# Attention scores: three PSUM banks for the row maxima, and the subtraction of the maxima in 32-row products at the ends of each burst

## The chip, the cores and the metric

One Trainium2 chip (trn2), one core of it. The metric is the device time of one execution in microseconds (us); the kernel before is given by the median of three runs.

## The reference, cut to what matters

x has 8 batches of 1024 rows of 256; there are 16 heads of 64 (DHEAD).

```python
def _L0_attn_ref(x, gamma, Wq, Wkv, W_bilinear, Wo):
    ...
    q = apply_rotary(q, cos, sin) * DHEAD ** (-0.5)
    k = apply_rotary(k, cos, sin)
    kt = jnp.einsum('bhnd,hde->bhne', k, W_bilinear)
    sim = jnp.einsum('bhid,bhjd->bhij', q, kt)
    attn = jax.nn.softmax(sim, axis=-1)
    out = jnp.einsum('bhij,bhjd->bhid', attn, v)
    ...
x = x + _L0_attn_ref(_layernorm(x, axis=-1), ...)
x = x + _L0_ffn_ref(_layernorm(x, axis=-1), ...)
```

## The kernel before, in words

The program has four parts: the weights are prepared, the input is normalised and turned, the attention runs (most of the time), and a feed-forward part ends it. The change lies in the attention, in `attention()`.

Attention works on pairs of heads, T = 64 pairs (8 batches of 8 pairs). The two heads of a pair lie in partitions 0-63 and 64-127 (`rows(e)`), so that two products of 64 rows, one for each head, can run side by side. The order of work is written out by hand: each engine has its own list, `span(k, t, b)`, and engines meet only in semaphores. A span does three things at once for three different pairs: the attention of pair t (`attn`), the row maxima of pair t+1 (`prep`), and the projections of pair t+2 (`proj`). `pairs` puts spans 1 to 56 in a loop of eight spans per turn.

A span has four quarters q. On TensorE a quarter is:

- a burst over four key tiles n = 4q to 4q+3. For each tile and each head e there are four products into a scores bank S[e][n % 2] (`score`, parts 0 to 3): q_hi with k_hi, q_hi with k_lo, q_lo with k_hi, and `neg_max` with `ones_rows`, which subtracts the maxima (L624). For the next pair there is one product each into X[0] or X[1] (`max_score`, L641), whose row maximum VectorE takes from the bank (L562). A bank X[e] is free again when VectorE has reduced it.
- projections (q = 0 keys, 1 queries, 2 values, L692 and L707) or, at q = 3, the bilinear product of the keys (L721), the first half into bank M ("shared" in the rows), the second into X[0], and at q = 3 also the turning of the maxima (L725) into X[1];
- at q = 0 and 2 the sums of the probabilities over partitions (`sums`, L647, bank M), and always the four tiles' products with the values (L753), called PV below.

ScalarE (ACT) makes the probabilities (`exp`, L491) as soon as a scores bank is complete. At q = 3 it makes, behind the last `exp`, in this order: q_hi (L506), the first half of k_hi (L511), the high part of the maxima (L517), the second half of k_hi. GpSimd (POOL) adds the probabilities over tiles (L435), adds the swapped halves for the rotary embedding (L441) and scales the output (L447).

The maxima of a pair lie in a column layout. Their high and low parts (`nmt`, "neg_max_parts") are made at the end of span t-1, and SyncE (SP) copies them by DMA into rows of `NM` ("neg_max"): row 64e + part. The product of L624 waits for these DMAs at n = 0 (`nm_in`):

```python
for part, made in enumerate((nm_hi, nm_lo)):
    wait(sp, made, t + 2)
    at_rest()
    for e in two:
        row = e * DH + part
        sp.dma_start(NM[(k + 1) % 2][row:row + 1, :].bitcast(F), ...).then_inc(nm_in, 16)
```

Of the kernel before, what the change touches and what calls it, by code (L numbers as in the profile page):

```python
# [12 lines left out]
P = 128  # L13
# [256 lines left out]
def attention(nc, cos_in, sin_in, ident_in, xt_scr, w_scr, wb_scr, z_scr, XT, W, V, cos, next_loads):  # L270
    with ExitStack() as ctx:
# [11 lines left out]
        prob = [sb(f"prob{e}", [P, RING, HALF], F) for e in two]  # L283
        psums = [[sb(f"prob_sum{e}{h}", [P, HALF], F) for h in two] for e in two]
# [21 lines left out]
        exped, x_red, added = per_head("probs_made"), per_head("max_reduced"), per_head("probs_added")  # L306
# [10 lines left out]
        CONSTS = 16 * 4 + 8  # L317
# [24 lines left out]
        def _(sp):  # L342
# [20 lines left out]
            def swap(x, t, c):  # L363
                wait(sp, sin_made[x], 2 * (t + 2) + c + 1)
                at_rest()
                wait(sp, rot_made[x], 2 * (t + 2) + c - 1)
# [50 lines left out]
        def _(pool):  # L417
            for s in added + rot_made + [z_made]:
                pool.sem_inc(s, CREDIT)
# [3 lines left out]
            def add(t, n):  # L423
# [3 lines left out]
                for e in (1, 0):  # L427
                    wait(pool, exped[e], 16 * t + n + 1)
                    if j == 1:
                        wait(pool, l_made, 4 * (t - 1) + 2 * half + 2)  # L430
                        a = prob[e][:, (n - 1) % RING, :]
                    else:
                        wait(pool, added[e], 14 * t + adds_by(n - 1))
                        a = psums[e][half][:, :]
                    nc.gpsimd.tensor_tensor(psums[e][half][:, :], a, prob[e][:, n % RING, :], ALU.add).then_inc(added[e], 1)  # L435

            def rope(t, x, c):
                done = 2 * (t + 2) + c + 1
                wait(pool, swap_in[x][c], 32 * (t + 3))
                wait(pool, cos_made[x], done)  # L440
                nc.gpsimd.tensor_tensor(rot[x][:, cols(c)], rot[x][:, cols(c)], swapped[x][:, cols(c)], ALU.add)\  # L441
                    .then_inc(rot_made[x], 1)
# [6 lines left out]
            def span(k, t, b):  # L449
                attn, prep, proj = has(k)  # L450
                for q in range(QUADS):
                    for jj in range(4):
# [6 lines left out]
                        if proj and q in (1, 2) and jj in (1, 3):  # L459
                            rope(t, q - 1, jj // 2)  # L460
# [4 lines left out]
        def _(act):  # L465
# [10 lines left out]
            def span(k, t, b):  # L476
                attn, prep, proj = has(k)
                u = k % 2
                for q in range(QUADS):
# [4 lines left out]
                    for jj in range(4):  # L484
                        n = 4 * q + jj
                        for e in (1, 0):
                            if attn:
                                wait(act, s_made[e], 16 * t + n + 1)
                                wait(act, pv_made[e], 16 * t + n - RING + 1)
                                wait(act, added[e], 14 * t + adds_by(n) - 7)  # L490
                                nc.scalar.activation(prob[e][:, n % RING, :], S[e][n % 2][:, :], ACT.Exp).then_inc(exped[e], 1)  # L491
# [9 lines left out]
                    if q == 3:  # L501
                        if proj:
                            wait(act, rot_made[Q], 2 * (t + 2) + 2)
# [10 lines left out]
                        if prep:  # L514
                            wait(act, nm_turned, t + 2)
                            wait(act, nm_in, 64 * (t + 1))
# [7 lines left out]
        def _(dve):  # L524
# [4 lines left out]
            for k, p in enumerate(prob):  # L529
                nc.vector.memset(p[:, :, :], 0.0).then_inc(const, 1)  # L530
# [3 lines left out]
            for e in two:  # L534
                nc.vector.memset(onesr[e * DH:e * DH + 2, :].bitcast(F), 1.0).then_inc(const, 1)
# [17 lines left out]
            def span(k, t, b):  # L553
                attn, prep, proj = has(k)
                u = k % 2
                for q in range(QUADS):
                    for jj in range(4):
                        n = 4 * q + jj
                        for e in two:
                            if prep:  # L560
                                wait(dve, x_made[e], 16 * (t + 1) + n + 1)
                                nc.vector.reduce_max(mx[1 - u][:, e, n // 2, n % 2:n % 2 + 1], X[e][:, :], axis=AX.X)\  # L562
# [34 lines left out]
        def _(pe):  # L597
# [3 lines left out]

            def score(t, u, n, e, part):

                half, j = n // 8, n % 8
                out = S[e][n % 2][:, :]
                keys, q = slice(j * P, (j + 1) * P), cols(half)
                if part == 0:
                    wait(pe, exped[e], 16 * t + n - 1)
# [3 lines left out]
                    nc.tensor.matmul(out, KH[u][rows(e), keys], QH[u][rows(e), q], start=True, stop=False)  # L612
# [4 lines left out]
                elif part == 2:  # L617
                    if n == 0:
                        wait(pe, lo_made[Q], t + 1)
                    nc.tensor.matmul(out, KH[u][rows(e), keys], QL[u][rows(e), q], start=False, stop=False)  # L620
                else:
                    if n == 0:
                        wait(pe, nm_in, 64 * (t + 1))
                    nc.tensor.matmul(out, onesr[rows(e), :], NM[u][rows(e), q], start=False, stop=True).then_inc(s_made[e], 1)  # L624

            def max_score(k, t, v, n, e):

                wait(pe, x_red[e], 16 * (t + 1) + n)
                if n == 0:
                    wait(pe, hi_made[K], 2 * (t + 1) + 2)  # L630
                    wait(pe, hi_made[Q], t + 2)
                    wait(pe, lo_made[K], 2 * (t + 1) + 2)
                    wait(pe, nm_lo, t + 1)
                if e == 0 and has(k)[2]:
                    if n == 4 or n == 8:
                        x = n // 4 - 1
                        wait(pe, sin_made[x], 2 * (t + 2) + 2)
                    if n == 12:
                        wait(pe, v_copied, 2 * (t + 2) + 2)
                tile, part = n // 2, n % 2  # L640
                nc.tensor.matmul(X[e][:, :], QH[v][rows(e), tile * P:(tile + 1) * P], KH[v][rows(e), cols(part)],  # L641
                                 start=True, stop=True).then_inc(x_made[e], 1)

            def sums(t, h):
                for e in two:
                    wait(pe, added[e], 14 * t + 7 * h + 7)
                    nc.tensor.matmul(M[rows(e), :], ones[:, :], psums[e][h][:, :], start=True, stop=True).then_inc(l_made, 1)  # L647

            def span(k, t, b):
# [6 lines left out]
                for q in range(QUADS):  # L656
                    for jj in range(4):
                        n = 4 * q + jj
                        if attn:
                            for part in two:  # L660
                                for e in two:
                                    score(t, u, n, e, part)
                        if prep:
                            max_score(k, t, 1 - u, n, 0)
                        if attn:
                            score(t, u, n, 1, 2)
                            score(t, u, n, 0, 2)
                            score(t, u, n, 1, 3)
                            score(t, u, n, 0, 3)
                        if prep:  # L670
                            max_score(k, t, 1 - u, n, 1)

                    if proj and q < 2:
                        for c in two:
                            out = (M if c == 0 else X[0])[:, :]
                            if q == K and c == 0:
# [4 lines left out]
                                wait(pe, hi_made[K], 2 * (t + 1) + 1)  # L681
                                wait(pe, lo_made[K], 2 * (t + 1) + 1)
                            elif q == Q and c == 0:
                                wait(pe, sin_made[K], 2 * pp + 1)
                                wait(pe, inv_made, 2 * (t - 1) + 2)
# [9 lines left out]
                    if proj and q == 2:  # L695
                        for c in two:
                            bank = M if c == 0 else X[0]
                            if c == 0:
                                wait(pe, sin_made[Q], 2 * pp + 1)
# [10 lines left out]
                    if q == 3:  # L710
                        if proj:
                            for c in two:
                                wait(pe, rot_made[K], 2 * pp + c + 1)
                                if c == 0:
                                    wait(pe, v_copied, 2 * pp + 1)
                                    wait(pe, inv_made, 2 * t + 1)
# [10 lines left out]
                    if attn:  # L727
                        if q == 0 and k >= 1:
                            if proj:
                                wait(pe, sin_made[K], 2 * pp + 1)  # L730
                            else:
                                if prep:
                                    wait(pe, lo_made[K], 2 * (t + 1) + 1)
                                wait(pe, inv_made, 2 * (t - 1) + 1)
                            sums(t - 1, 1)
                        if q == 2:
                            if proj:
                                wait(pe, v_copied, 2 * pp + 1)
                            else:
                                wait(pe, inv_made, 2 * (t - 1) + 2)  # L740
                            sums(t, 0)
                        half = q // 2
                        for jj in range(4):
                            n = 4 * q + jj
                            j = n % 8
                            for e in two:
# [6 lines left out]
                                nc.tensor.matmul(O[rows(e), :], V[k // 2 % 2][:, j, col:col + DH], prob[e][:, n % RING, :],  # L753
# [412 lines left out]
```

## Time and profile before

| | |
|---|---|
| median of 3 runs | 4118.36 us (4116.03 to 4121.81) |
| the profiled execution's own time | 4126.92 us |
| its span in the profile | 4124.7 us, mean granted TensorE clock 0.986 |
| TensorE busy | 3712.5 us, 90% of the span |
| VectorE, ScalarE, GpSimd busy | 72%, 42%, 71% |

Attention takes the profile from about 450 to 3520 us, and the pattern of a span repeats in it. TensorE's matmuls are pipelined, so the start of one and the start of the next are the numbers to compare; the duration of one reaches over the start of the next. A granted clock of 1.0 is 2.4 GHz, 0.5 is 1.2 GHz. "issue" is idle time that the profile puts down to no other engine.

### The profile page before, as it was taken

What the parts mean: (1) busy time and instruction counts of PE and PEld (TensorE: products, weight loads), DVE (VectorE), ACT (ScalarE), POOL (GpSimd) and SP (SyncE); (2) the same over time, 40 slices, a digit from 0 to 9 for tenths busy, and PEclk for the clock granted to TensorE, in tenths of its full rate; (3) what the DMA queues carried; (4) which work ended last, traced back from release to release, by engine and by line L of the source; (5) the groups of instructions that cost most, each with busy time, mean ns of one, the idle gap of its engine ahead of it and who ended that gap; (6) DMA issues with size and microseconds to landing.
All of it is one profiled execution on the core that took longest, in us unless ns stands there. A gap on an engine that the chain in (4) does not pass through costs nothing. (4 is left out here: it accounts for less than half of the span.)

```text
span 4124.7 us, 72584 instructions
## 1 busy us (share of the span) xinstructions
PE 3712.5 (90%) x22106; PEld 2378.9 (58%) x22106; DVE 2985.7 (72%) x4457; ACT 1718.4 (42%) x3109; POOL 2915.3 (71%) x2407
## 2 busy tenths in 40 slices
PE   0114999999999999999999999999999999799999
PEld 0002555555655655555555655655656555488888
DVE  4555677777777777677777767776777777399998
ACT  1000344444444444444444444444444444355555
POOL 0111788888888888888888888888888889522221
PEclk9998999999999999999999999999999999899999
DMA  5222111111111111111111111121111101233332
GB/s 203 100 92 111 54 48 70 47 48 52 70 53 48 47 68 47 48 47 70 48 49 51 70 48 52 47 78 48 52 68 50 50 34 46 79 98 93 98 99 72
DMA packets 180740, 273.57 MB, mean 66 GB/s; under 512 B 18720, under 2 KB 113568, under 8 KB 173984
## 3 DMA queue, kind: packets, MB, share of 16 engines
q1 hardware_dynamic: 162720, 244.06, 16.8%
q10 hardware_dynamic: 17664, 25.17, 1.7%
q8 instruction: 174, 2.85, 0.3%
q14 instruction: 182, 1.49, 0.1%
HBM read 131.28 MB, written 69.73 MB: 49 GB/s over the span
## 5 line engine op out<-in xcount | busy, mean ns | idle before, releaser
L435 POOL TENSOR_TENSOR prob_sum<-prob_sum,prob 128x512 f32<-128x512 f32 x1536 | 1983.9, 1324 | 271.5 <-ACT prob L491 269.2
L562 DVE TENSOR_REDUCE row_max<-max_scores 128x1 f32<-128x512 f32 x2048 | 1322.9, 688 | 461.4 <-PE max_scores L641 453.3
L491 ACT ACTIVATE prob<-scores 128x512 f32<-128x512 f32 x2048 | 1111.0, 596 | 1099.2 <-PE scores L624 1083.7
L641 PE MATMUL max_scores<-k_hi,q_hi 64*128 64x512 f32 x2048 | 949.1, 465 | 12.9 <-DVE k_lo L591 4.8
L753 PE MATMUL attn_out<-prob,v 128*64 128x512 f32 x4096 | 929.4, 596 | 0.0
L620 PE MATMUL scores<-q_lo,k_hi 64*128 64x512 f32 x2048 | 641.7, 407 | 0.0
L624 PE MATMUL scores<-neg_max,ones_rows 64*128 64x512 f32 x2048 | 613.9, 400 | 12.5 <-issue 9.3
L541 DVE RECIPROCAL sum_inverted<-shared 128x512 f32<-128x512 f32 x128 | 429.6, 3356 | 256.9 <-PE shared L647 256.7
L753 PEld LDWEIGHTS attn_out<-prob,v 128*64 128x64 f32 x4096 | 285.5, 137 | 561.8 <-issue 560.2
L612 PE MATMUL scores<-q_hi,k_hi 64*128 64x512 f32 x2048 | 514.0, 433 | 8.6 <-issue 7.6
L641 PEld LDWEIGHTS max_scores<-k_hi,q_hi 64*128 64x128 f32 x2048 | 382.5, 187 | 235.5 <-DVE row_max L562 127.6
L616 PE MATMUL scores<-q_hi,k_lo 64*128 64x512 f32 x2048 | 468.4, 396 | 0.0
L435 POOL TENSOR_TENSOR prob_sum<-prob 128x512 f32<-128x512 f32 x256 | 324.4, 1290 | 129.5 <-ACT prob L491 129.5
L624 PEld LDWEIGHTS scores<-neg_max,ones_rows 64*128 64x128 f32 x2048 | 359.8, 187 | 50.8 <-DMA neg_max<-neg_max_parts 15.7
L612 PEld LDWEIGHTS scores<-q_hi,k_hi 64*128 64x128 f32 x2048 | 214.0, 187 | 237.2 <-issue 215.8
L888 POOL TENSOR_TENSOR up_scale<-veps_b,halfpow 128x1 f32<-128x1 f32 x64 | 35.1, 549 | 426.3 <-DVE up_biased L1017 400.9
L620 PEld LDWEIGHTS scores<-q_lo,k_hi 64*128 64x128 f32 x2048 | 321.0, 187 | 12.1
L474 ACT ACTIVATE z_stage<-attn_out 128x512 f32<-128x512 f32 x128 | 76.6, 598 | 545.3 <-PE attn_out L753 541.3
L230 PE MATMUL xt_bank<-ident,x_twice 128*128 128x128 f32 x128 | 31.4, 428 | 278.8 <-DVEq L213 278.8
L616 PEld LDWEIGHTS scores<-q_hi,k_lo 64*128 64x128 f32 x2048 | 253.8, 189 | 10.2
L692 PE MATMUL shared<-xt_batch,w_group 128*128 128x512 f32 x768 | 216.1, 418 | 23.2 <-DMA xt_batch<-x_turned_parts 23.2
L692 PE MATMUL max_scores<-xt_batch,w_group 128*128 128x512 f32 x768 | 198.6, 395 | 0.0
(122 smaller groups left out, 4742.7 us busy)
## 6 DMA issues: line engine op xcount, KB each, us to landing
w_group<-w_parts SPq DMA_DIRECT2D x32, 1536.0 KB, 6.6
k_swapped<-sin_products SPq DMA_DIRECT2D x256, 128.0 KB, 2.1
q_swapped<-sin_products SPq DMA_DIRECT2D x256, 128.0 KB, 2.0
attn_normalised<-z_stage SPq DMA_DIRECT2D x128, 256.0 KB, 2.1
v<-attn_normalised SPq DMA_DIRECT2D x64, 512.0 KB, 4.1
x_turned_parts<-xt_parts ACTq DMA_DIRECT2D x16, 1024.0 KB, 4.5
xt_batch<-x_turned_parts SPq DMA_DIRECT2D x8, 2048.0 KB, 10.7
x_in<-in_x SPq DMA_DIRECT2D x16, 512.0 KB, 3.7
```

Source lines behind the costliest of these rows:

```text
L435: nc.gpsimd.tensor_tensor(psums[e][half][:, :], a, prob[e][:, n % RING, :], ALU.add).then_inc(added[e], 1)
L474: nc.scalar.activation(zst[h][:, :], O[:, :], ACT.Copy).then_inc(z_copied, 1)
L491: nc.scalar.activation(prob[e][:, n % RING, :], S[e][n % 2][:, :], ACT.Exp).then_inc(exped[e], 1)
L541: nc.vector.reciprocal(inv[:, :], M[:, :]).then_inc(inv_made, 1)
L562: nc.vector.reduce_max(mx[1 - u][:, e, n // 2, n % 2:n % 2 + 1], X[e][:, :], axis=AX.X)\
L612: nc.tensor.matmul(out, KH[u][rows(e), keys], QH[u][rows(e), q], start=True, stop=False)
L616: nc.tensor.matmul(out, KL[u][rows(e), keys], QH[u][rows(e), q], start=False, stop=False)
L620: nc.tensor.matmul(out, KH[u][rows(e), keys], QL[u][rows(e), q], start=False, stop=False)
L624: nc.tensor.matmul(out, onesr[rows(e), :], NM[u][rows(e), q], start=False, stop=True).then_inc(s_made[e], 1)
L641: nc.tensor.matmul(X[e][:, :], QH[v][rows(e), tile * P:(tile + 1) * P], KH[v][rows(e), cols(part)], start=True, stop=True).then_inc(x_made ...
L692: last = nc.tensor.matmul(out, w[:, wp, kt, base:base + P], XT[:, xp, kt, cols(c)], start=m == 0, stop=m == len(order) - 1)
L753: nc.tensor.matmul(O[rows(e), :], V[k // 2 % 2][:, j, col:col + DH], prob[e][:, n % RING, :], start=j == 0, stop=j == 7).then_inc(pv_made[ ...
```

## The change

1. `max_score` writes to three banks in turn instead of two: X[0], X[1] and M (`bank_of`). Since M also serves the projections and the sums, TensorE gets new waits on `x_red[1]` before them.
2. Part 3 of `score` goes. In its place `shift` makes the same subtraction with 32 rows for two tiles and both heads, four products in a row on four groups of 32 rows. For the first two tiles of a burst it opens the accumulation (before the scores), for the last two it closes it (behind the last `max_score`). `NM` and `ones_rows` hold the two parts in rows 32g and 32g+1 of all four groups, so there are eight DMAs per pair, not four.
3. The probabilities of both heads lie in one tile; GpSimd adds both heads in one operation of 1024 columns, and the rotary addition takes 1024 columns at once, at jj = 2.

```diff
+        def bank_of(n, e):
+            return (X[0], X[1], M)[(2 * (n % 4) + e) % 3]
...
@@ sync: span
-                        for e in two:
-                            row = e * DH + part
-                            sp.dma_start(NM[(k + 1) % 2][row:row + 1, :].bitcast(F),
-                                         nmt[e * TILES:(e + 1) * TILES, part, :].bitcast(F)).then_inc(nm_in, 16)
+                        for g in two:
+                            row = 32 * g + part
+                            for e in two:
+                                sp.dma_start(NM[(k + 1) % 2][row + e * DH:row + e * DH + 1, :].bitcast(F),
+                                             nmt[e * TILES:(e + 1) * TILES, part, :].bitcast(F)).then_inc(nm_in, 16)
@@ gpsimd: add, rope
-                for e in (1, 0):
+                for e in two:
                     wait(pool, exped[e], 16 * t + n + 1)
...
-                    nc.gpsimd.tensor_tensor(psums[e][half][:, :], a, prob[e][:, n % RING, :], ALU.add).then_inc(added[e], 1)
+                nc.gpsimd.tensor_tensor(psums[half][:, :, :], a, prob[:, n % RING, :, :], ALU.add).then_inc(added, 1)
...
+                nc.gpsimd.tensor_tensor(rot[x][:, :], rot[x][:, :], swapped[x][:, :], ALU.add).then_inc(rot_made[x], 1)
@@ tensor
+            def shift(t, u, n, first):
+                if n == 0:
+                    wait(pe, nm_in, 128 * (t + 1))
+                for m in (n, n + 1):
+                    for e in two:
+                        if first:
+                            wait(pe, exped[e], 16 * t + m - 1)
+                        r = slice(e * DH + 32 * (m % 2), e * DH + 32 * (m % 2) + 32)
+                        last = nc.tensor.matmul(S[e][m % 2][:, :], onesr[r, :], NM[u][r, cols(m // 8)], start=first, stop=not first)
+                        if not first:
+                            last.then_inc(s_made[e], 1)
...
-                    if n == 0:
-                        wait(pe, nm_in, 64 * (t + 1))
-                    nc.tensor.matmul(out, onesr[rows(e), :], NM[u][rows(e), q], start=False, stop=True).then_inc(s_made[e], 1)
+                    last = nc.tensor.matmul(out, KH[u][rows(e), keys], QL[u][rows(e), q], start=False, stop=first)
+                    if first:
+                        last.then_inc(s_made[e], 1)
 
             def max_score(k, t, v, n, e):
-                wait(pe, x_red[e], 16 * (t + 1) + n)
+                i, q, pp = 2 * (n % 4) + e, n // 4, t + 2
+                if i >= 3:
+                    wait(pe, x_red[1 - e], 16 * (t + 1) + 4 * q + (i - 3) // 2 + 1)
...
@@ tensor: span
                         if attn:
-                            for part in two:
+                            if jj == 0:
+                                shift(t, u, n, True)
+                            for part in range(3):
                                 for e in two:
                                     score(t, u, n, e, part)
                         if prep:
-                            max_score(k, t, 1 - u, n, 0)
-                        if attn:
-                            score(t, u, n, 1, 2)
-                            score(t, u, n, 0, 2)
-                            score(t, u, n, 1, 3)
-                            score(t, u, n, 0, 3)
-                        if prep:
-                            max_score(k, t, 1 - u, n, 1)
+                            for e in two:
+                                max_score(k, t, 1 - u, n, e)
+                        if attn and jj == 3:
+                            shift(t, u, n - 1, False)
...
                                 wait(pe, lo_made[K], 2 * (t + 1) + 1)
+                                wait(pe, x_red[1], 16 * (t + 1) + 3)
```

The last added wait stands ahead of the key projection into M; the other projections into M have one like it.

What moves, in the order of the two programs. The subtraction is `scores<-neg_max,ones_rows`, the products for the maxima are `max_scores<-k_hi,q_hi`. TensorE, the last tile of the last burst of a span, before:

```order
L612 MATMUL scores<-q_hi,k_hi 128x512 x2
L616 MATMUL scores<-q_hi,k_lo 128x512 x2
L641 MATMUL max_scores<-k_hi,q_hi 128x512
L620 MATMUL scores<-q_lo,k_hi 128x512 x2
L624 MATMUL scores<-neg_max,ones_rows 128x512 x2
L641 MATMUL max_scores<-k_hi,q_hi 128x512
L721 MATMUL shared<-k_rotated,wb_blocks 128x512
```

TensorE, the same place now:

```order
L629 MATMUL scores<-q_hi,k_hi 128x512 x2
L633 MATMUL scores<-q_hi,k_lo 128x512 x2
L637 MATMUL scores<-q_lo,k_hi 128x512 x2
L675 MATMUL max_scores<-k_hi,q_hi 128x512 x2
L614 MATMUL scores<-neg_max,ones_rows 128x512 x4
L757 MATMUL shared<-k_rotated,wb_blocks 128x512
```

The subtraction for the third and fourth tile (the last x4) now stands behind all eight products of the maxima, directly ahead of the bilinear product. TensorE, the first two tiles of a burst now, behind PV of the burst before:

```order
L791 MATMUL attn_out<-prob,v 64x512 x8
L614 MATMUL scores<-neg_max,ones_rows 128x512 x4
L629 MATMUL scores<-q_hi,k_hi 128x512 x2
L633 MATMUL scores<-q_hi,k_lo 128x512 x2
L637 MATMUL scores<-q_lo,k_hi 128x512 x2
L675 MATMUL max_scores<-k_hi,q_hi 128x512 x2
L629 MATMUL scores<-q_hi,k_hi 128x512 x2
L633 MATMUL scores<-q_hi,k_lo 128x512 x2
L637 MATMUL scores<-q_lo,k_hi 128x512 x2
L675 MATMUL shared<-k_hi,q_hi 128x512
L675 MATMUL max_scores<-k_hi,q_hi 128x512
```

The product that reads `neg_max` has moved from behind three pairs of products to the very front. SP's DMA queue at the end of a span, before:

```order
L406 DMA neg_max<-neg_max_parts 1x8x128 [waits max_hi]
L406 DMA neg_max<-neg_max_parts 1x8x128
L406 DMA neg_max<-neg_max_parts 1x8x128 [waits max_lo]
L406 DMA neg_max<-neg_max_parts 1x8x128
L369 DMA k_swapped<-sin_products 64x512 [waits k_sin_made,k_rot_made]
```

and now:

```order
L411 DMA neg_max<-neg_max_parts 1x8x128 [waits max_hi]
L411 DMA neg_max<-neg_max_parts 1x8x128 x3
L411 DMA neg_max<-neg_max_parts 1x8x128 [waits max_lo]
L411 DMA neg_max<-neg_max_parts 1x8x128 x3
L373 DMA k_swapped<-sin_products 64x512 [waits k_sin_made,k_rot_made]
```

The same queue issues eight DMAs of the same size where it issued four.

## Rows read from the trace of the kernel before

**Rows 1.** Busy time by stretch, steady attention: us, busy us per engine, clock, DMA.

```profile
1000.00:3500.00 2500.00, 2480.18 (x14447) 1479.65 (x14447) 1830.25 (x2381) 1106.48 (x2030) 2195.69 (x1726) 0.99 0.15 53
```

**Rows 2.** Costliest groups, whole profile: line, engine, operation, count, busy, mean ns, idle.

```profile
L435 POOL TENSOR_TENSOR prob_sum<-prob_sum,prob 128x512 f32<-128x512 f32 x1536 | 1983.9, 1324 | 271.5 <-ACT prob L491 269.2
L562 DVE TENSOR_REDUCE row_max<-max_scores 128x1 f32<-128x512 f32 x2048 | 1322.9, 688 | 461.4 <-PE max_scores L641 453.3
```

**Rows 3.** Timeline of TensorE, last burst of a span and the next: start, length.

```profile
1003.62 1.46 PE L753 MATMUL attn_out<-prob,v 128*64 128x512 f32 x6
1005.00 0.50 PE L612 MATMUL scores<-q_hi,k_hi 64*128 64x512 f32 x2
1005.34 0.39 PE L616 MATMUL scores<-q_hi,k_lo 64*128 64x512 f32 x2
1005.57 0.39 PE L641 MATMUL max_scores<-k_hi,q_hi 64*128 64x512 f32 x1
...
1009.90 0.49 PE L641 MATMUL max_scores<-k_hi,q_hi 64*128 64x512 f32 x1
1010.32 1.13 PE L721 MATMUL shared<-k_rotated,wb_blocks 128*128 128x512 f32 x2
...
1012.35 3.65 PE L753 MATMUL attn_out<-prob,v 128*64 128x512 f32 x16
1015.93 0.50 PE L612 MATMUL scores<-q_hi,k_hi 64*128 64x512 f32 x2
...
1016.94 0.50 PE L624 MATMUL scores<-neg_max,ones_rows 64*128 64x512 f32 x2
...
1021.53 0.50 PE L692 MATMUL shared<-xt_batch,w_group 128*128 128x512 f32 x1
```

**Rows 4.** Timeline of TensorE, where the other bursts begin and end.

```profile
1029.09 0.50 PE L612 MATMUL scores<-q_hi,k_hi 64*128 64x512 f32 x2
...
1034.42 1.66 PE L692 MATMUL shared<-xt_batch,w_group 128*128 128x512 f32 x6
...
1040.95 0.50 PE L612 MATMUL scores<-q_hi,k_hi 64*128 64x512 f32 x2
...
1046.29 1.69 PE L707 MATMUL shared<-w_group,xt_batch 128*128 128x256 f32 x12
...
1053.79 0.49 PE L612 MATMUL scores<-q_hi,k_hi 64*128 64x512 f32 x2
```

**Rows 5.** Timeline of VectorE in the last burst of two spans.

```profile
1006.00 5.13 DVE L562 TENSOR_REDUCE row_max<-max_scores 128x1 f32<-128x512 f32 x8 [0.84 <-PE max_scores L641]
...
2046.25 1.29 DVE L562 TENSOR_REDUCE row_max<-max_scores 128x1 f32<-128x512 f32 x2
```

**Rows 6.** Timeline of ScalarE at the end of the span of rows 3.

```profile
1010.16 1.09 ACT L491 ACTIVATE prob<-scores 128x512 f32<-128x512 f32 x2 [0.20 <-PE scores L624]
1011.13 1.06 ACT L506 ACTIVATE q_hi<-q_rotated 128x1024 fp32r<-128x1024 f32 x1
1012.08 0.60 ACT L511 ACTIVATE k_hi<-shared 128x512 fp32r<-128x512 f32 x1
1012.55 0.25 ACT L517 ACTIVATE neg_max_parts<-max_scores 16x128 fp32r<-16x128 f32 x1
```

**Rows 7.** The DMAs of the maxima: SP's issues, all issues (ns min/median/max), who waits.

```profile
1012.90 2.88 SPq L406 DMA_DIRECT2D neg_max<-neg_max_parts  x4
...
L406 SPq DMA_DIRECT2D neg_max<-neg_max_parts x256: 623/655/2701, 420.5 to 3520.8; - x128
...
1016.93 0.19 PEld L624 LDWEIGHTS scores<-neg_max,ones_rows 64*128 64x128 f32 x2 [0.25 <-DMA neg_max<-neg_max_parts]
```

**Rows 8.** Timeline of TensorE at a turn of the loop.

```profile
2052.93 0.60 PE L612 MATMUL scores<-q_hi,k_hi 64*128 64x512 f32 x2 [0.50 <-issue]
...
2056.18 0.58 PE L624 MATMUL scores<-neg_max,ones_rows 64*128 64x512 f32 x1 [1.89 <-issue]
...
2062.95 0.51 PE L692 MATMUL shared<-xt_batch,w_group 128*128 128x512 f32 x1
```

**Rows 9.** Busy time by stretch at the same place, columns as in rows 1.

```profile
2055.00:2062.00 7.00, 5.82 (x27) 5.62 (x28) 3.28 (x5) 2.55 (x6) 2.19 (x2) 0.53 0.02 6
```

More of the change, by code:

```diff
@@ L282, in attention @@
         WB = sb("wb_blocks", [P, PAIRS, P], F)
-        prob = [sb(f"prob{e}", [P, RING, HALF], F) for e in two]
-        psums = [[sb(f"prob_sum{e}{h}", [P, HALF], F) for h in two] for e in two]
+        prob = sb("prob", [P, RING, 2, HALF], F)
+        psums = [sb(f"prob_sum{h}", [P, 2, HALF], F) for h in two]
         prod = sb("sin_products", [P, N], F)
@@ L365, in swap @@
                 at_rest()
-                wait(sp, rot_made[x], 2 * (t + 2) + c - 1)
+                wait(sp, rot_made[x], t + 2)
                 at_rest()
@@ L426, in add, with rope @@
                     return
-                for e in (1, 0):
+                for e in two:
                     wait(pool, exped[e], 16 * t + n + 1)
[L429 to L434, printed above, removed]
-                    nc.gpsimd.tensor_tensor(psums[e][half][:, :], a, prob[e][:, n % RING, :], ALU.add).then_inc(added[e], 1)
[L437 to L442, printed above, removed]
+                if j == 1:
+                    wait(pool, l_made, 4 * (t - 1) + 2 * half + 2)
+                    a = prob[:, (n - 1) % RING, :, :]
+                else:
+                    wait(pool, added, 14 * t + adds_by(n - 1))
+                    a = psums[half][:, :, :]
+                nc.gpsimd.tensor_tensor(psums[half][:, :, :], a, prob[:, n % RING, :, :], ALU.add).then_inc(added, 1)
+            def rope(t, x):
+                for c in two:
+                    wait(pool, swap_in[x][c], 32 * (t + 3))
+                wait(pool, cos_made[x], 2 * (t + 2) + 2)
+                nc.gpsimd.tensor_tensor(rot[x][:, :], rot[x][:, :], swapped[x][:, :], ALU.add).then_inc(rot_made[x], 1)
             def norm_z(t, h):
@@ L533, in _ @@
             dve.wait_ge(zeroed, 1)
-            for e in two:
-                nc.vector.memset(onesr[e * DH:e * DH + 2, :].bitcast(F), 1.0).then_inc(const, 1)
+            for g in range(4):
+                nc.vector.memset(onesr[32 * g:32 * g + 2, :].bitcast(F), 1.0).then_inc(const, 1)
             dve.wait_ge(const, CONSTS)
@@ L607, in score @@
                 if part == 0:
-                    wait(pe, exped[e], 16 * t + n - 1)
+                    if not first:
+                        wait(pe, exped[e], 16 * t + n - 1)
                     if n == 0:
@@ L611, in score @@
                         wait(pe, hi_made[K], 2 * t + 2)
-                    nc.tensor.matmul(out, KH[u][rows(e), keys], QH[u][rows(e), q], start=True, stop=False)
+                    nc.tensor.matmul(out, KH[u][rows(e), keys], QH[u][rows(e), q], start=not first, stop=False)
                 elif part == 1:
@@ L630, in max_score @@
                     wait(pe, hi_made[K], 2 * (t + 1) + 2)
-                    wait(pe, hi_made[Q], t + 2)
                     wait(pe, lo_made[K], 2 * (t + 1) + 2)
+                elif q == 0 and i == 1:
                     wait(pe, nm_lo, t + 1)
[L634 to L639, printed above, removed]
+                elif q and i == 1:
+                    wait(pe, x_red[1], 16 * (t + 1) + 4 * q)
+                elif q and not proj:
+                    wait(pe, x_red[i // 2], 16 * (t + 1) + 4 * q - i // 2)
+                    if q == 1 and i == 2:
+                        wait(pe, inv_made, 2 * (t - 1) + 2)
+                    if q == 3 and i == 2:
+                        wait(pe, inv_made, 2 * t + 1)
+                elif q and i == 0:
+                    if q < 3:
+                        wait(pe, sin_made[q - 1], 2 * pp + 2)
+                    else:
+                        wait(pe, v_copied, 2 * pp + 2)
+                elif q == 1:
+                    wait(pe, sin_made[K], 2 * pp + 1)
+                    wait(pe, inv_made, 2 * (t - 1) + 2)
+                elif q == 2:
+                    wait(pe, sin_made[Q], 2 * pp + 1)
+                elif q == 3:
+                    wait(pe, v_copied, 2 * pp + 1)
+                    wait(pe, inv_made, 2 * t + 1)
@@ L640, in max_score @@
                 tile, part = n // 2, n % 2
-                nc.tensor.matmul(X[e][:, :], QH[v][rows(e), tile * P:(tile + 1) * P], KH[v][rows(e), cols(part)],
+                nc.tensor.matmul(bank_of(n, e)[:, :], QH[v][rows(e), tile * P:(tile + 1) * P], KH[v][rows(e), cols(part)],
                                  start=True, stop=True).then_inc(x_made[e], 1)
@@ L645, in sums @@
                 for e in two:
-                    wait(pe, added[e], 14 * t + 7 * h + 7)
-                    nc.tensor.matmul(M[rows(e), :], ones[:, :], psums[e][h][:, :], start=True, stop=True).then_inc(l_made, 1)
+                    wait(pe, added, 14 * t + 7 * h + 7)
+                    nc.tensor.matmul(M[rows(e), :], ones[:, :], psums[h][:, e, :], start=True, stop=True).then_inc(l_made, 1)
             def span(k, t, b):
@@ L698, in span @@
                             if c == 0:
-                                wait(pe, sin_made[Q], 2 * pp + 1)
+                                if not prep:
+                                    wait(pe, sin_made[Q], 2 * pp + 1)
+                                wait(pe, x_red[1], 16 * (t + 1) + 11)
                             else:
```

52 lines of the change are left out of this document (27 added, 25 removed).

## The prediction

> **What bounds the kernel now.** I read the busy time by stretch first. In steady attention TensorE is busy for 2480.18 of 2500 us, POOL for 2195.69 and VectorE for 1830.25 [rows 1]: whatever makes TensorE stand still is paid in full, and what POOL and VectorE save is worth nothing by itself. Then TensorE's timeline shows where its time goes. A span is 48.79 us, from the last burst of one (1005.00) to that of the next (1053.79) [rows 3, 4]. The bursts take 5.32 (q = 3), 5.60 (q = 0), 5.33 and 5.34 us, each from its first product to the first projection [rows 3, 4]; projections, sums and PV between them take 7.56, 6.53 and 7.50 us. A burst isn't a stream of products alone: VectorE reduces its eight maxima in 5.13 us almost without a pause [rows 5]. So inside a burst VectorE and TensorE are about level.
>
> The chain at the end of a span comes third. The last `exp` pair starts 5.16 us into the last burst, then q_hi, k_hi, the maxima's high part at 12.55 [rows 6], and SP's four DMAs from 12.90 on [rows 7]. The weight load of the subtraction in the next burst starts at 1016.93, after 0.25 us of idle time that the DMA ended [rows 7]. That is 1.00 us after the burst's first product [rows 3]: the maxima already come just in time, and only because three pairs of products stand ahead of the one that reads them.
>
> **The change, part by part.** *Slots removed.* Pairs of products start 0.23 us apart (1005.34 to 1005.57) [rows 3]. A burst has 20 such slots; now it has 16, and two for the subtractions if four products of 32 rows run as two of 64 rows do. 2 x 0.23 x 4 bursts would be 1.8 us a span, if slots bound the burst.
>
> *What bounds the new burst.* The first product of a burst starts 0.52 us after the last pair of PV (PV pairs are 0.43 apart, so the third of the row of six is at 1004.48), and the next slot comes 0.34 behind it. The first projection comes 0.42 us behind the last product for the maxima (1009.90, 1010.32) [rows 3]. Where the array changes from one shape to another, a slot of 0.23 becomes about 0.42 and the one behind it 0.34. The new burst has two more such places, 32 to 64 rows at its start and 64 to 32 at its end. No row shows 32 rows; between 0 and 0.30 us a place, I take what these rows show. The Trainium skill says the same of this change (TensorEngine Tiling (Array Packing), "Key Properties": switching the tiling mode drains the array, switching the tile doesn't). By that rule the burst below is 5.63 us; if a switch between 32 and 64 rows cost nothing, 5.20.
>
> From the burst's start: scores at 0.42, 0.76 and 0.99, the first maxima at 1.22. VectorE starts 0.43 after its product (1005.57 to 1006.00) [rows 3, 5], so at 1.65, and back to back one reduction follows another in 0.60 (1.29 less 0.69) [rows 2, 5]. With three banks the eighth product needs the fifth reduction: 1.65 + 4 x 0.60 + 0.69 = 4.74, so it starts at 4.79. The closing subtraction starts at 5.21, the projection at 5.63. Its bank M is free at 1.65 + 5 x 0.60 + 0.69 = 5.34, so the new wait on M is covered, but only by 0.3 us. So the burst does not get shorter, it grows: the first maxima stand one slot and one change of shape later than before (1.22 against 0.57). Three bursts, 16.89 us, replace 16.27: **+0.6 us** up to the last burst.
>
> *The closing subtraction on ScalarE.* Third and fourth tile are complete only at the burst's end: 5.21 + 0.50 + 0.11 gives 5.82 for the first of four `exp`, 0.49 apart, so the last pair starts at 6.80 and not at 5.16. Everything behind it on ScalarE, k_hi and the high part of the maxima, is late by **1.64 us**. PV needs these tiles only after two pairs of it; that is covered.
>
> *Four more DMAs.* The four take 2.88 us with a last one of 0.66, so 0.74 each [rows 7]. They are issued one after another on SP: four more are **+2.96 us**. Bounds: 0.62 (the shortest issue) to 0.80 each. From the last issue (1012.90 + 2.88 - 0.66 = 1015.12) to the weight load there are 1.81 us, unchanged. What stands behind them on SP, a store of z and the next swap (needed some 9 us into the next span), is covered by its own distance.
>
> *The subtraction in front.* Before, the load came 11.93 us after the start of the last burst, and the next burst began at 10.93. Now it comes at 11.93 + 1.64 + 2.96 = 16.53, and the burst begins with it. That step is +5.60 us, and with +0.62 the span is 55.0 us: **+6.2 us**. TensorE stands still for about 5.3 us in each, since PV ends 3.6 us after 7.7. 63 such steps are 391 us.
>
> *The clock.* At a turn of the loop TensorE idles for 1.89 us and more, and then the granted clock is 0.53 of full for 7 us, its lower level [rows 8, 9]; that burst took 10.02 us, of which 2.3 between two products of one pair, so 7.7 against 5.60 [rows 3, 8]. An idle time of 5.3 us should do so in every span. If the low level reaches 3 us into the burst, the first maxima come 1 us later and VectorE passes that on; if over the whole burst, it costs 2.5. I take **1.5 us**, 95 us in all. The turns of the loop lie inside the new wait now, and their low clock is already counted: 7 x 4.4 = 31 us back.
>
> *POOL.* One operation of 1024 columns for two of 512: between 2 x 1.32 [rows 2] and about half. POOL has idle time and gets more of it, since the span grows; I take nothing. Without that cover it would be the sums at q = 0 and 2 that wait. Rotary additions in one piece, at jj = 2: needed at q = 3, nothing. The larger constants at the start: under 2 us, nothing.
>
> Sum: 391 + 95 - 31 = 455 us on the profiled execution's 4126.92, 4582; the median lies 8.6 below that execution. **4575 us**, 11% slower.
>
> **Rivals.** *A: no cost of shape.* The Tiling page would be wrong for 64 to 32 rows. Bursts 5.20, closing subtraction at 4.83: 3 x 0.43 + 0.38 = 1.67 us less a span, 4470 us. For it: both shapes keep all 128 columns. Against it: every change the rows show has its gap.
>
> *B: the clock holds.* Then 95 us go: 4480. Against it stand rows 8 and 9, with less than half the idle time.
>
> *C: the clock is low over the whole next burst.* 2.5 us a span and not 1.5: 4640.
>
> *D: four products of 32 rows don't run together,* but in two pairs. Then each burst has two more slots of 0.23: about 1.6 us a span over three and a half bursts, 4675.
>
> *E: the maxima arrive in time after all,* if the eight DMAs are issued beside each other or PV hides them. Then bursts decide, and by A's 5.20 they are 0.2 us shorter than before: 4 x 0.2 x 63 = 50 us, **4068 us, faster**. It decides where the last DMA lands within 11.2 us of the last burst's start; the sum has it at 16.5, and the four of today land at 11.9. All that speaks for it is the count of slots.
>
> *F: gain and loss cancel,* within 0.2%, which is about what a measurement of this kernel can tell from no change. No row leads there.
>
> **How the numbers follow.** Forecast 0.52, A 0.12, B 0.11, C 0.13, D 0.07, E 0.03, F 0.02. The range holds all but E and F and a rest of the tails: from 4440 (A with shorter issues, 0.62 each) to 4690 (D). Faster 0.03, same 0.02, slower 0.95.
>
> **What would show it.** In the profile after: the first waits of a span's first burst are of the subtraction's weight load on the DMA of `neg_max`, some 4 to 6 us in each span, where it was 0.25; SP shows eight issues of 0.7 us; a granted clock that falls once a span; bursts of 5.5 to 5.7 us away from that place, the first reduction 1.6 us after their start; gaps of about 0.42 around the closing four. The forecast is wrong if that load waits less than 2 us, if the span stays below 52 us, or if the bursts fall under 5.2.

## The result, and the profile after

| | before | after |
|---|---|---|
| median | 4117.93 us (4 runs) | 4595.22 us (4594.78 to 4597.28, 4 runs) |
| ratio | | 1.116, 95% interval 1.1144 to 1.1175 |
| span of the profile, mean granted clock | 4124.7 us, 0.986 | 4593.0 us, 0.951 |

The change makes the kernel 11.6% slower. Busy time by stretch in steady attention, after (as [rows 1]):

```profile
1000.00:3900.00 2900.00, 2638.37 (x14545) 1495.26 (x14543) 1836.08 (x2398) 1067.25 (x2040) 2098.38 (x919) 0.94 0.13 47
```

TensorE is busy for 91% of the stretch, where it was 99%. The groups of the profile's page say where it stands still, and that GpSimd's joint addition takes 2450 ns where two single ones took 2 x 1324 [rows 2]:

```profile
L440 POOL TENSOR_TENSOR prob_sum<-prob_sum,prob 128x1024 f32<-128x1024 f32 x768 | 1882.0, 2450 | 462.7 <-ACT prob L495 433.2
L614 PE MATMUL scores<-neg_max,ones_rows 32*128 32x512 f32 x2048 | 282.8, 528 | 324.1 <-DMA neg_max<-neg_max_parts 324.1
```

TensorE's timeline over the end of one span and the start of the next (as [rows 3]):

```profile
1082.48 2.31 PE L791 MATMUL attn_out<-prob,v 128*64 128x512 f32 x10
1084.73 0.51 PE L614 MATMUL scores<-neg_max,ones_rows 32*128 32x512 f32 x4
1085.17 0.50 PE L629 MATMUL scores<-q_hi,k_hi 64*128 64x512 f32 x2
1085.50 0.40 PE L633 MATMUL scores<-q_hi,k_lo 64*128 64x512 f32 x2
1085.73 0.39 PE L637 MATMUL scores<-q_lo,k_hi 64*128 64x512 f32 x2
1085.97 0.39 PE L675 MATMUL max_scores<-k_hi,q_hi 64*128 64x512 f32 x2
...
1089.96 0.50 PE L614 MATMUL scores<-neg_max,ones_rows 32*128 32x512 f32 x4
1090.39 1.13 PE L757 MATMUL shared<-k_rotated,wb_blocks 128*128 128x512 f32 x2
...
1092.41 3.65 PE L791 MATMUL attn_out<-prob,v 128*64 128x512 f32 x16
1101.09 1.06 PE L614 MATMUL scores<-neg_max,ones_rows 32*128 32x512 f32 x4 [5.02 <-DMA neg_max<-neg_max_parts]
1102.07 0.80 PE L629 MATMUL scores<-q_hi,k_hi 64*128 64x512 f32 x2
...
1103.52 0.63 PE L675 MATMUL max_scores<-k_hi,q_hi 64*128 64x512 f32 x2
...
1108.72 1.65 PE L725 MATMUL shared<-xt_batch,w_group 128*128 128x512 f32 x6
```

Read from the burst's start at 1084.73: 0.44 to the first scores, then 0.33, 0.23, the first maxima at 1.24, the closing four at 5.23, the next shape at 5.66. PV ends, TensorE does nothing for 5.02 us, and the burst behind it takes 7.63 us. ScalarE and SP at the end of that span (as [rows 6, 7]):

```profile
1090.61 2.07 ACT L495 ACTIVATE prob<-scores 128x512 f32<-128x512 f32 x4 [2.27 <-PE scores L614]
1092.53 1.08 ACT L510 ACTIVATE q_hi<-q_rotated 128x1024 fp32r<-128x1024 f32 x1
1093.48 0.62 ACT L515 ACTIVATE k_hi<-shared 128x512 fp32r<-128x512 f32 x1
1093.95 0.25 ACT L521 ACTIVATE neg_max_parts<-max_scores 16x128 fp32r<-16x128 f32 x1
```

```profile
1094.30 5.55 SPq L411 DMA_DIRECT2D neg_max<-neg_max_parts  x8
```

The high part of the maxima is made 9.22 us into the last burst (7.55 before), the eight issues take 5.55 us (2.88 before), and the first product that waits starts at 16.36. Busy time around the landing (as [rows 9]):

```profile
1083.00:1090.00 7.00, 7.00 (x50) 3.87 (x46) 5.50 (x8) 2.07 (x4) 5.17 (x4) 1.00 0.39 163
1100.00:1107.00 7.00, 5.91 (x30) 4.66 (x32) 2.40 (x4) 2.17 (x4) 0.12 (x1) 0.54 0.11 40
```

The granted clock is 1.00 in the last burst and 0.54 around the landing; pairs start 0.43 us apart there, the 1.2 GHz level.

### The profile page after: what moved, and what is told of

It reads as the page before. It is cut to its first block and busy times, and to the rows that moved or that the text cites. A ratio compares the mean times of both kernels' runs of the same rounds, so it can differ in the third digit from the quotient of the medians.

```text
span 4593.0 us, 71326 instructions
## 1 busy us (share of the span) xinstructions
PE 3879.2 (84%) x22106; PEld 2378.2 (52%) x22106; DVE 2970.1 (65%) x4458; ACT 1663.2 (36%) x3109; POOL 2776.2 (60%) x1383
## 5 line engine op out<-in xcount | busy, mean ns | idle before, releaser
L440 POOL TENSOR_TENSOR prob_sum<-prob_sum,prob 128x1024 f32<-128x1024 f32 x768 | 1882.0, 2450 | 462.7 <-ACT prob L495 433.2
L565 DVE TENSOR_REDUCE row_max<-max_scores 128x1 f32<-128x512 f32 x1536 | 988.4, 683 | 855.8 <-PE max_scores L675 854.8
L440 POOL TENSOR_TENSOR prob_sum<-prob 128x1024 f32<-128x1024 f32 x128 | 305.1, 2384 | 548.2 <-ACT prob L495 548.2
L675 PE MATMUL max_scores<-k_hi,q_hi 64*128 64x512 f32 x1536 | 551.0, 451 | 10.8 <-DVE k_lo L594 4.3
L614 PE MATMUL scores<-neg_max,ones_rows 32*128 32x512 f32 x2048 | 282.8, 528 | 324.1 <-DMA neg_max<-neg_max_parts 324.1
L637 PE MATMUL scores<-q_lo,k_hi 64*128 64x512 f32 x2048 | 468.4, 423 | 0.0
L614 PEld LDWEIGHTS scores<-neg_max,ones_rows 32*128 32x128 f32 x2048 | 110.5, 192 | 599.4 <-issue 551.6
L565 DVE TENSOR_REDUCE row_max<-shared 128x1 f32<-128x512 f32 x512 | 349.4, 682 | 19.2 <-PE shared L675 17.9
L675 PEld LDWEIGHTS max_scores<-k_hi,q_hi 64*128 64x128 f32 x1536 | 254.9, 202 | 184.4 <-DVE row_max L565 142.6
L675 PE MATMUL shared<-k_hi,q_hi 64*128 64x512 f32 x512 | 236.3, 461 | 0.3
```

What stands on the lines that cost most here:

```text
L440: nc.gpsimd.tensor_tensor(psums[half][:, :, :], a, prob[:, n % RING, :, :], ALU.add).then_inc(added, 1)
L614: last = nc.tensor.matmul(S[e][m % 2][:, :], onesr[r, :], NM[u][r, cols(m // 8)], start=first, stop=not first)
L637: last = nc.tensor.matmul(out, KH[u][rows(e), keys], QL[u][rows(e), q], start=False, stop=first)
L675: nc.tensor.matmul(bank_of(n, e)[:, :], QH[v][rows(e), tile * P:(tile + 1) * P], KH[v][rows(e), cols(part)], start=True, stop=True).then_i ...
```

## The experiments

Ten kernels ran, each beside the kernel before, which ran again with them. Its median was 4120.56 us beside the runs with four DMAs, with 64 rows, with the early closing and with three banks in the old order; 4121.08 beside the one with both remedies and the last one; 4123.82 beside the other four. Counts and means over spans, here and below, are of the stretch from 1000 to 3300 us.

**Four DMAs instead of eight, in the changed kernel.**

```diff
                         for g in two:
                             row = 32 * g + part
-                            for e in two:
-                                sp.dma_start(NM[...][row + e * DH:row + e * DH + 1, :], nmt[e * TILES:(e + 1) * TILES, part, :])
+                            sp.dma_start(NM[...][row:row + DH + 1:DH, :], nmt[:, part, :])
```

> The changed kernel with four DMAs of the maxima per pair instead of eight: one DMA writes both heads' rows of one group and part, same data, same bytes. Theory 1 (the chain q_hi, k_hi, high part of the maxima, eight issues one after another on SP, landing, first product of the next span sets the span): four issues of about 0.70 us less, so the idle time ahead of a span's first burst falls from 5.1 to about 2.4 us, bursts elsewhere stay at 5.66 us; 2.7 x 63 = 170 us less, about 4425 us if the clock still falls in each span, about 4330 if it no longer does. Theory 2 (bursts and the new waits on the third bank are the cost, the DMAs lie beside them): no change, 4595 us.

4317.02 us, 278 less than the change; ratio 1.0476 (1.0458 to 1.0493), mean clock 0.981. Timelines of TensorE and SP:

```profile
1304.69 3.65 PE L790 MATMUL attn_out<-prob,v 128*64 128x512 f32 x16
1310.31 0.61 PE L613 MATMUL scores<-neg_max,ones_rows 32*128 32x512 f32 x4 [1.96 <-DMA neg_max<-neg_max_parts]
...
1316.09 1.67 PE L724 MATMUL shared<-xt_batch,w_group 128*128 128x512 f32 x6
```

```profile
1306.57 2.35 SPq L410 DMA_DIRECT2D neg_max<-neg_max_parts  x4
```

The issues end 3.2 us earlier in the span, the idle time falls from 5.02 to 1.96 us, and the burst behind it from 7.63 to 5.78 us in this span, where the clock held. Theory 2 is out. The gain is larger than either value expected: 3.1 us less idle time are 195 us, and the other 83 are put down to the clock. It now falls in 22 of 43 spans and for a shorter time, where in the change it falls in every one, and the first burst of a span takes 6.3 us on the mean instead of 7.6, which is some 80 us.

**Eight DMAs in the kernel before.**

```diff
-                        for e in two:
-                            row = e * DH + part
+                        for e, row in ((0, part), (1, DH + part), (0, 32 + part), (1, 96 + part)):
```

> The kernel before with eight DMAs of the maxima per pair instead of four; the four added ones copy the same data into rows 32, 33, 96 and 97 of neg_max, against which ones_rows is zero. Nothing else moves. Theory 1: the last issue comes 2.85 us later, the subtraction of the first tile, three pairs into the burst, waits 3.0 us instead of 0.2; 183 us more, 4300 us if the granted clock holds, 4376 us if it falls in each span as it does in the changed kernel. Theory 2 (the DMAs lie beside other work, the change loses elsewhere): 4118 us.

4326.78 us, ratio 1.0499 (1.0481 to 1.0516), clock 0.974. TensorE's timeline shows the wait in the middle of the first burst, where the subtraction then stood:

```profile
1314.17 3.65 PE L752 MATMUL attn_out<-prob,v 128*64 128x512 f32 x16
1318.29 0.60 PE L611 MATMUL scores<-q_hi,k_hi 64*128 64x512 f32 x2 [0.47 <-issue]
...
1321.72 0.51 PE L623 MATMUL scores<-neg_max,ones_rows 64*128 64x512 f32 x2 [2.17 <-DMA neg_max<-neg_max_parts]
```

Four added DMAs of 4 KB, whose data meets zeros, cost 5% by themselves. The time lies between the two values of theory 1, and the clock falls in 30 of 44 spans. Theory 2 is out here too.

**The first subtraction of a span behind its scores,** in the changed kernel.

```diff
-                            if jj == 0:
+                            if jj == 0 and q:
                                 shift(t, u, n, True)
                             for part in range(3):
                                 for e in two:
                                     score(t, u, n, e, part)
+                            if n == 1:
+                                shift(t, u, 0, False)
```

> The changed kernel, but in the first burst of a span (q = 0) the subtraction for the first two tiles closes the accumulation behind their scores instead of opening it, so that the product that reads neg_max stands behind seven slots and not in front. Eight DMAs and all else as in the change. Theory 1: the DMAs land at the same time (16.4 us after the last burst's start), TensorE does some 1.9 us of work before it waits for them, so the idle time falls from 5.1 to about 3.2 us; behind the landing ScalarE's four exp hold up tile 3, so that 4.5 to 5.2 us of the burst are left instead of 7.6; 1.2 to 2.4 us less a span, 4445 to 4520 us, 4480 the likeliest. If the place of the reading product does not matter: 4595 us.

4512.91 us, 82 less than the change; ratio 1.0950 (1.0932 to 1.0969). The wait is still in TensorE's timeline, but shorter, and behind work:

```profile
1304.22 3.65 PE L793 MATMUL attn_out<-prob,v 128*64 128x512 f32 x16
...
1312.82 0.51 PE L614 MATMUL scores<-neg_max,ones_rows 32*128 32x512 f32 x4 [3.11 <-DMA neg_max<-neg_max_parts]
...
1314.68 0.80 PE L629 MATMUL scores<-q_hi,k_hi 64*128 64x512 f32 x2 [0.91 <-ACT prob L495]
...
1318.46 1.67 PE L727 MATMUL shared<-xt_batch,w_group 128*128 128x512 f32 x6
```

5.64 us of the burst are left behind the landing in this span instead of 7.63 (6.1 on the mean, against 7.6), but more than the 4.5 to 5.2 expected, so the time lies at the slow end of the forecast. Two things fill the rest: 0.91 us of waiting for ScalarE's `exp`, and the low clock, which still falls in nearly every span.

**Both remedies.** The two edits above together.

> Both remedies in the changed kernel: four DMAs of the maxima (4317 us alone) and the subtraction of the first two tiles of a span behind their scores (4513 us alone). What is left of the change is its bursts and ScalarE's delay. Theory 1: the landing, 13.2 us after the last burst's start, now meets TensorE at the place where it gets to by itself (11.3 + 1.9), the wait and the low clock go; the first burst takes some 6.4 us, since ScalarE's four exp hold up tile 3, the others 5.66; 1.8 us a span more than the kernel before, 4230 us. Rival (four products of 32 rows and their order cost nothing once the maxima arrive in time): 4120 us or less.

4231.14 us, ratio 1.0268 (1.0251 to 1.0285), clock 0.991. TensorE's timeline has no wait for the DMAs left that lasts microseconds:

```profile
1333.12 3.65 PE L792 MATMUL attn_out<-prob,v 128*64 128x512 f32 x16
1338.57 0.51 PE L613 MATMUL scores<-neg_max,ones_rows 32*128 32x512 f32 x4
...
1340.44 0.51 PE L628 MATMUL scores<-q_hi,k_hi 64*128 64x512 f32 x2 [0.93 <-ACT prob L494]
...
1342.86 0.51 PE L613 MATMUL scores<-neg_max,ones_rows 32*128 32x512 f32 x4
1343.30 1.65 PE L726 MATMUL shared<-xt_batch,w_group 128*128 128x512 f32 x6
```

What is left, 110 us, is longer bursts. Three of a span take 5.66 us instead of 5.33, some 60 us in all. The first takes 6.60 us here instead of 5.60, mostly because TensorE now waits 0.93 us for ScalarE's `exp` in every span: that is the price of reading the maxima later, and the change itself does not pay it. So of the change's 477 us at least 364 hung on the arrival of the maxima, the low clock behind it included.

**Products of 64 rows for the subtraction,** same places, eight DMAs; `ones_rows` is zero in the groups that are not used.

```diff
-                        r = slice(e * DH + 32 * (m % 2), e * DH + 32 * (m % 2) + 32)
+                        r = rows(e)
```

> The changed kernel, its opening and closing subtractions made of products of 64 rows (two pairs at each end instead of four side by side), eight DMAs as before in it; the array's row shape no longer changes inside a burst. Theory 1 (a change between 32 and 64 rows costs about 0.19 us before and 0.11 us behind): two slots of 0.23 more and two changes of shape of 0.30 less cancel, bursts of 5.6 to 5.75 us as now, 4590 us within 15. Rival A (a change between 32 and 64 rows costs nothing, the four products save two slots): bursts 0.46 us longer, 1.6 us a span, about 4700 us.

4581.33 us, ratio 1.1126 (1.1107 to 1.1144), 14 us under the change. TensorE's timeline of the last burst of a span:

```profile
1311.23 0.73 PE L614 MATMUL scores<-neg_max,ones_rows 64*128 64x512 f32 x4
...
1316.06 0.95 PE L614 MATMUL scores<-neg_max,ones_rows 64*128 64x512 f32 x4
1316.94 1.13 PE L757 MATMUL shared<-k_rotated,wb_blocks 128*128 128x512 f32 x2
```

The burst takes 5.71 us, 0.05 more than with 32 rows, and not 0.46: four products of 32 rows do run together (in the change their starts lie within 0.01 us, here the opening pairs stand 0.33 apart), and the two changes of shape take back nearly all of it. Rival A is out. The run is a little faster than the change all the same: its first closing pair starts at 4.83 us and not at 5.23, and the high part of the maxima is made 0.2 us earlier, at 9.01.

**The closing subtraction ahead of the last maxima,** in the changed kernel.

```diff
                                     score(t, u, n, e, part)
+                            if jj == 3:
+                                shift(t, u, n - 1, False)
                         if prep:
                             for e in two:
                                 max_score(k, t, 1 - u, n, e)
-                        if attn and jj == 3:
-                            shift(t, u, n - 1, False)
```

> The changed kernel with the closing subtraction ahead of the last two products for the maxima instead of behind them. Theory 1: the closing four start about 4.4 us into the burst and not 5.2, so ScalarE's last four exp and with them the high part of the maxima come 0.8 us earlier; the burst ends by the sixth reduction (5.4 us) and not by the closing four; 3 x 0.25 + 0.8 = 1.6 us less a span, about 4495 us. If the delay on ScalarE is not on the path that sets the span: 0.75 us a span at most, about 4550 us. If the bursts do not shorten because of one more change of shape, but ScalarE's delay counts: 4545 us with bursts still 5.66.

4559.77 us, 35 less than the change; ratio 1.1068 (1.1050 to 1.1087). This expectation missed: by its time the run lies next to the second case (4550, ScalarE's delay not on the path), by its rows next to the third (4545, bursts hardly shorter, the delay counts). TensorE's and ScalarE's timelines:

```profile
1306.33 0.51 PE L614 MATMUL scores<-neg_max,ones_rows 32*128 32x512 f32 x4
...
1311.06 0.50 PE L614 MATMUL scores<-neg_max,ones_rows 32*128 32x512 f32 x4
1311.92 1.13 PE L757 MATMUL shared<-k_rotated,wb_blocks 128*128 128x512 f32 x2
```

```profile
1315.06 0.25 ACT L521 ACTIVATE neg_max_parts<-max_scores 16x128 fp32r<-16x128 f32 x1
```

The closing four start at 4.73, not 4.4, since I had left out the gap of their own change of shape, and a third change, back to 64 rows for the last maxima, ends the burst at 5.59 instead of 5.66. ScalarE's high part came 0.5 us earlier (8.73 us into the burst, against 9.22), not 0.8, and the product that waits for the DMAs starts 0.5 us earlier too. 0.5 + 3 x 0.07 = 0.7 us a span is 45 us, near the 35 measured; the bursts alone would be 13. So ScalarE's delay is on the path. This run took back 0.5 us of it; at the same rate the whole 1.67 us would be some 105 us, an estimate that no run here tests.

**Three banks and joint additions in the old order,** the subtraction as it was, four DMAs.

```diff
-                nc.tensor.matmul(X[e][:, :], QH[v][rows(e), tile * P:(tile + 1) * P], KH[v][rows(e), cols(part)],
+                nc.tensor.matmul(bank_of(n, e)[:, :], QH[v][rows(e), tile * P:(tile + 1) * P], KH[v][rows(e), cols(part)],
```

> Only parts 1 and 3 of the change: three banks for the maxima, and GpSimd's additions for both heads at once; the subtraction stays one pair of 64-row products per tile in the old places, four DMAs, the old order. Theory 1 (two banks held TensorE and VectorE in step, and the new order lost what the third bank gives): the first maxima stay 0.57 us into the burst, the sixth reduction ends at 4.7, TensorE needs 20 slots of 0.23 and two changes of shape, so bursts of 5.0 us instead of 5.33; about 1.3 us less a span, 4035 us. Rival (VectorE's eight reductions bind whatever the banks): bursts stay 5.3 us, 4118 us. Rival (the new waits on M are paid): bursts over 5.4 us, slower than 4118.

4025.03 us, **faster** than before: ratio 0.9774 (0.9758 to 0.9790). TensorE's timeline, last burst of a span and the next:

```profile
1317.51 0.49 PE L614 MATMUL scores<-q_hi,k_hi 64*128 64x512 f32 x2
...
1318.07 0.39 PE L662 MATMUL max_scores<-k_hi,q_hi 64*128 64x512 f32 x1
...
1322.48 1.12 PE L746 MATMUL shared<-k_rotated,wb_blocks 128*128 128x512 f32 x2
...
1328.09 0.50 PE L614 MATMUL scores<-q_hi,k_hi 64*128 64x512 f32 x2
...
1329.21 0.49 PE L626 MATMUL scores<-neg_max,ones_rows 64*128 64x512 f32 x2
```

The burst takes 4.97 us against 5.32 [rows 3]. Both rivals of this run are out: the third bank was worth something, and the waits on M are covered.

**Joint additions alone,** two banks. (The edit is the third part of the change.)

> Only part 3 of the change: GpSimd adds both heads in one operation of 1024 columns and the rotary additions take 1024 columns; two banks, old order, four DMAs. Theory 1: GpSimd's work is covered, 4118 us within 8, and the whole gain of the three banks (4025 us) is the banks'. Rival: the joint additions, 2.45 us against 2 x 1.32, free sums and probabilities earlier and carry part of the gain: 4060 to 4105 us.

4115.35 us, ratio 0.9986 (0.9976 to 0.9995): 0.14%, for 0.2 us less GpSimd work per pair of additions. Covered, as expected; the gain of the run above is the third bank's.

**Three banks, joint additions and two DMAs.**

```diff
-                        for e in two:
-                            row = e * DH + part
-                            sp.dma_start(NM[...][row:row + 1, :], nmt[e * TILES:(e + 1) * TILES, part, :])
+                        sp.dma_start(NM[...][part:part + DH + 1:DH, :], nmt[:, part, :])
```

> Three banks and joint additions in the old order (4025 us), and two DMAs of the maxima per pair: one DMA writes both heads' rows of one part. In the run with four DMAs the subtraction of the first tile still starts 1.11 us into the first burst and not 0.80, 1.79 us behind the last issue. Theory 1 (that wait is still the DMAs'): the last issue comes 1.4 us earlier, the wait is gone, bursts at q = 0 go from 5.46 to about 5.0 us; 0.35 x 63 = 22 us less, 4003 us. If something else holds that burst: 4025 us.

3996.06 us, ratio 0.9695 (0.9679 to 0.9711). SP's timeline, and TensorE's first subtraction of the next span:

```profile
1312.85 1.26 SPq L408 DMA_DIRECT2D neg_max<-neg_max_parts  x2
```

```profile
1316.56 0.62 PE L624 MATMUL scores<-neg_max,ones_rows 64*128 64x512 f32 x2
```

The subtraction starts 3.0 us behind the last issue now, so the DMAs no longer hold it. 29 us instead of 22.

**The same with separate additions.** (The third part of the change is taken back.)

> Three banks and two DMAs in the old order, with GpSimd's additions left as before the change, one head and 512 columns at a time. Theory 1 (GpSimd is covered here too: 14 x 2.65 + 6 x 1.30 = 44.9 us of work in a span of 47.3): 3996 to 4005 us. Rival (with the span shorter by 1.5 us GpSimd's additions come too late for the sums or for ScalarE's ring of eight): 4015 us or more.

3996.26 us, ratio 0.9693 (0.9677 to 0.9709). The joint additions are worth nothing here either. Three banks and one DMA per part are all that a better kernel needs of this.

## Why the prediction was right

4575 was forecast, 4595.22 measured. Its steps:

- *Bursts of 5.63 us.* 5.66 measured, with slots of 0.44, 0.33 and 0.23, first maxima at 1.24 (1.22), closing four at 5.23 (5.21). The last product for the maxima (1089.53) and the closing four (1089.96) stand 0.43 us apart, not 0.23, and the run with 64 rows gave the price from the other side. The Trainium skill says that a change of tiling mode drains the array (TensorEngine Tiling (Array Packing), "Key Properties"), and this trace agrees for 32 against 64 rows. Rival A falls with it, and D with the starts of the closing four, all within 0.01 us.
- *ScalarE late by 1.64 us.* 9.22 less 7.55 is 1.67.
- *Four more DMAs, 2.96 us.* 5.55 less 2.88 is 2.67 for the issues here; the runs with four and eight DMAs, in either kernel, moved as it said. An added issue took 0.67 us, between the shortest (0.62) and the sum's 0.74.
- *Idle time of 5.3 us.* 5.02. The subtraction in front of the scores, shown by moving it, is worth 82 us with eight DMAs and 86 with four (4317 to 4231).
- *The clock, 1.5 us a span.* This term was sized too small. The first burst takes 7.63 us, not 5.66: 2.0 us, so the low level reaches well over half of the burst. The prediction's own reading at the turn of the loop, 7.7 against 5.60, was 2.1 and nearer than what it took. With 2.0 the sum is 0.5 us a span or 30 us higher; the DMAs' 0.3 us take 19 of them back. Of the 20 us between forecast and result that leaves some 9; 0.03 us more in each of three bursts and on ScalarE are nearly 8. That the forecast came within 20 us owes something to luck, since two errors point opposite ways. Rival B falls. C's 2.5 us was too much, by as far as 1.5 was too little.
- *GpSimd, nothing.* Shown by two pairs of runs.
- *Rival E,* the one that ends faster, wanted the last DMA landed 11.2 us behind the last burst's start, and it was 16.36; F falls too. But there was a gain in the bursts, by another way than E's: the third bank shortens a burst by 0.35 us if the first maxima stay at 0.57. I had seen only the loss from moving them to 1.22, and not that the two belong to different parts of the change.

## What to carry to other kernels

Price a small transfer by its issue and its landing, not by its bytes: four copies of 4 KB on one queue, behind the last value made and ahead of the first product that reads it, cost 5%. Before products are packed into a new array shape, set the slots saved against the gaps of the changes, and look at which product the next engine waits for. When a change bundles several ideas, time them apart: here one part gains 2%, 3% with fewer copies, inside a change that loses 12%.

## What I had not expected of the hardware

One DMA that writes two partitions from sixteen (8 KB) takes no more issue time than one that writes one from eight: four such issues took 2.35 us (median 0.55 each), where four single ones took 2.88 in the kernel before (median 0.66). And how much the clock takes depends steeply on the idle time. With 5 us in each span it fell in all of them (mean 0.951, 2.0 us lost in each), with 3.1 us and 0.9 more behind it in nearly all (0.956), with 2.2 to 2.9 us in 30 of 44 (0.974), with 1.9 to 2.8 us in 22 of 43 (0.981), and with both remedies in 2 of 45 (0.991). The length of the idle time alone does not decide it: in the run with four DMAs spans with 1.9 us of it stand on both sides.
